# Expert outputs added in DRAM: one output array instead of two, with per-tile waits taken from a table

## What is computed

```python
def _L0_ffn_ref(x, Wr, br, W1, b1, W2, b2):        # E = 8 experts, D = 256, H = 512
    xf = x.reshape(n, d)                             # n = 10368 tokens, after a layer norm
    probs = jax.nn.softmax(xf @ Wr.T + br, axis=-1)
    top2_prob, top2_idx = jax.lax.top_k(probs, 2)
    comb = jnp.zeros((n, e)).at[jnp.arange(n)[:, None], top2_idx].add(top2_prob)
    h = jax.nn.gelu(jnp.einsum('nd,edh->enh', xf, W1) + b1[:, None, :], approximate=False)
    o = jnp.einsum('enh,ehd->end', h, W2) + b2[:, None, :]
    return jnp.einsum('ne,end->nd', comb, o)         # each token: a sum of two weighed rows
...
t = t + _L0_ffn_ref(_ln_t(t), ...)                   # t: the tokens of x1
```

## Time and profile before

| | |
|---|---|
| median of 3 runs | 1621.7 us (1620.54 to 1624.31) |
| the profiled execution | 1627.32 us, its span 1625.6 us |
| until x1 is done | 754.6 us |
| routing stage, to the first tile's load | 754.6 to 1004.7 us |
| expert stage, to the first load of the tail | 1004.7 to 1537.9 us |
| tail: loads and additions, then the output | 1537.9 to 1599.2, to 1625.6 us |
| busy share PE, DVE, ACT, POOL | 81%, 67%, 47%, 35% |

### The profile page before, as it was taken

The page is one execution under the profiler, slowest core; times in us unless marked ns, Lnnn a source line. Parts: engine busy times, 40 slices in busy tenths (PEclk is TensorE's granted clock), DMA queues, the critical chain, the costliest instruction groups (busy, mean ns, idle before and its releaser), DMA issues.

```text
span 1625.6 us, 36996 instructions
## 1 busy us (share of the span) xinstructions
PE 1309.9 (81%) x9796; PEld 1078.3 (66%) x9797; DVE 1087.0 (67%) x2553; ACT 772.1 (47%) x1828; POOL 568.0 (35%) x561
## 2 busy tenths in 40 slices
PE   0196999799999999986746501999999999999692
PEld 0186999756766666666746501888888888888531
DVE  6796555357888877874566662777777777777462
ACT  0294666344445444442576771455554545555200
POOL 0162111134433444330377775233333333333200
PEclk9997999889999999995555555999999999999896
DMA  8535566778778777661144354222222222222297
GB/s 321 139 92 192 202 241 235 252 176 188 188 170 202 179 185 189 162 148 54 54 150 135 131 179 158 76 85 91 91 91 87 84 89 90 90 91 77 85 423 310
DMA packets 258517, 251.16 MB, mean 155 GB/s; under 512 B 150009, under 2 KB 234446, under 8 KB 255204
## 3 DMA queue, kind: packets, MB, share of 16 engines
q1 hardware_dynamic: 238093, 197.20, 41.1%
q0 software_dynamic: 20320, 53.45, 9.6%
q10 hardware_dynamic: 66, 0.05, 0.0%
HBM read 152.34 MB, written 105.75 MB: 159 GB/s over the span
## 4 chain that ended last, share of the span: by engine, by line
PE 59%; DVE 15%; DMA 9%; issue 5%; ACT 5%; SPq 2%; POOL 2%; DVEq 0%; ACTq 0%; POOLq 0%
PE ps L690 15%; PE ps L675 14%; PE ps L490 5%; PE ps L470 4%; DMA u_d<-in_zstrings 3%; PE ps L659 2%; DMA pool_<-y_d 2%; PE ps L542 2%; POOL rows_d L1521 2%; PE ps L515 2%; SPq L288 2%; PE ps L525 2%; DMA pool_<-in_ffn_w 2%; ACT aux L1388 2%; PE ps L459 2%
## 5 line engine op out<-in xcount | busy, mean ns | idle before, releaser
L1530 POOL DMA_INDIRECT y_d<-pool_,to_s x176 | 173.5, 986 | 361.2 <-ACT pool_ L1447 331.9
L690 PE MATMUL ps<-pool_,aux 128*128 x2112 | 248.4, 274 | 6.2 <-DVE aux L1197 3.2
L675 PE MATMUL ps<-aux,pool_ 128*128 128x256 f16 x2112 | 246.5, 274 | 0.7 <-ACT aux L1440 0.6
L690 PEld LDWEIGHTS ps<-pool_,aux 128*128 128x128 f16 x2112 | 199.7, 98 | 49.9 <-issue 25.6
L675 PEld LDWEIGHTS ps<-aux,pool_ 128*128 x2112 | 206.2, 98 | 25.9 <-issue 1.7
L1521 POOL DMA_INDIRECT rows_d<-aux,idx_s x162 | 159.2, 983 | 105.4 <-ACT aux L1390 60.0
L1440 ACT ACTIVATE aux<-ps,b_s 128x256 f32<-128x256 f32 x352 | 138.3, 475 | 93.0 <-DVE aux L1197 92.6
L1432 ACT ACTIVATE aux<-ps 128x512 f16<-128x512 f32 x88 | 52.6, 597 | 188.8 <-PE ps L659 188.8
L1515 POOL DMA_DIRECT2D pool_<-v_d x64 | 50.0, 781 | 223.5 <-PE ps L575 220.3
L1205 DVE SCALAR_TENSOR_TENSOR pool_<-ps,pool_ 128x512 f32<-128x512 f32 x88 | 60.9, 692 | 96.0 <-PE ps L690 96.0
L515 PE MATMUL ps<-pool_,se_w_s 81*81 81x512 f32 x256 | 118.8, 608 | 6.1 <-DMA pool_<-k_d 6.1
(11 more groups left out here) (204 smaller groups left out, 3030.6 us busy)
## 6 DMA issues: line engine op xcount, KB each, us to landing
pool_<-rows_d SPq DMA_DIRECT2D x88, 260.0 KB, 2.8
pool_<-y_d SPq DMA_DIRECT2D x18, 1152.0 KB, 13.9
big<-in_x SPq DMA_DIRECT2D x2, 5184.0 KB, 21.3
xn_d<-big SPq DMA_DIRECT2D x16, 648.0 KB, 3.0
v_d<-aux SPq DMA_DIRECT2D x64, 162.0 KB, 2.1
ks_d<-aux SPq DMA_DIRECT2D x64, 162.0 KB, 2.2
pool_<-xn_d SPq DMA_DIRECT2D x32, 324.0 KB
pool_<-k_d SPq DMA_DIRECT2D x32, 324.0 KB
```

What stands on the lines that cost most here:

```text
L675: last = nc.tensor.matmul(o, w_s[:, a, bass.ds(e * (4 * PIECE) + (k * HID + j * 128), 128)], xh_s[:, par, b, k * SLOTS:(k + 1) * SLOTS], s ...
L690: last = nc.tensor.matmul(ps[:, 6 + par, s * C:(s + 1) * C], hh_s[:, par, a, j, s * 128:(s + 1) * 128], w_s[:, b, bass.ds(e * (4 * PIECE) ...
L1530: nc.gpsimd.indirect_dma_start(out=y_d[:, :], out_offset=bass.IndirectOffsetOnAxis(ap=to_s[:, par, k:k + 1], axis=0), in_=yo_s[:, par, k, ...
```

## The change

- `y_d` has one row for each token and 256 rows for padding (`TOKENS + SLOTS`). Both of a token's rows are added into the same row: the indirect DMA of `return_rows` has `compute_op=ALU.add`, and no bounds check.
- The array has to hold zeros first: ahead of b2 and the weights SP issues two DMAs that write `zero_s`, 1024 bytes a row, over all 10,624 rows of `y_d` (10.88 MB). DVE clears `zero_s` for that at the end of the first half instead of after the routing.
- Two additions to the same row must not be under way together. A token's two experts differ, so a tile waits for all tiles of the experts in front of its own: for each tile two more numbers stand in `tabi_s` (rows 2 and 3, nine more DVE instructions), the counts that `yst0` and `yst1` must have reached, at least 32 each. A tile past the last real one counts as an expert's first. POOL reads both numbers into registers for each tile from the third on, and waits on both semaphores.
- The tail loads one array: 9 loads instead of 18, 27 multiplications on PE instead of 54, and no L1238 on DVE.

The core of the diff:

```diff
-        y_d = dram("y_d", [2 * TOKENS, C])
+        y_d = dram("y_d", [TOKENS + SLOTS, C])
...
             sp.wait_ge(S["x1_c"], GROUPS + CREDIT)
+            sp.wait_ge(S["zero_c"], 1)
+            nought = zero_s[:, 0:1, 0:C]
+            sp.dma_start(y_d[0:TOKENS, :].rearrange("(b q) c -> b q c", q=HW),
+                         nought.to_broadcast([128, HW, C])).then_inc(S["nought"], 16)
+            sp.dma_start(y_d[TOKENS:, :].rearrange("(s b) c -> b s c", b=128),
+                         nought.to_broadcast([128, SLOTS // 128, C])).then_inc(S["nought"], 16)
             sp.dma_start(b2_s, bass.AP(ffn_b2.tensor, 0, [[0, 128], [1, EXPERTS * C]])).then_inc(S["b2_in"], 16)
...
-                for k in range(2):
-                    rows = y_d[k * TOKENS:(k + 1) * TOKENS, :].rearrange("(b q) c -> b q c", q=HW)
-                    sp.dma_start(got_s[:, n % 4, k], rows[:, n * CHUNK_P:(n + 1) * CHUNK_P, :]
-                                 ).then_inc(S[f"gat{n % 4}"], 16)
+                rows = y_d[0:TOKENS, :].rearrange("(b q) c -> b q c", q=HW)
+                sp.dma_start(got_s[:, n % 4, 0], rows[:, n * CHUNK_P:(n + 1) * CHUNK_P, :]
+                             ).then_inc(S[f"gat{n % 4}"], 16)
...
+            nc.vector.memset(zero_s[:, :, :], 0.0).then_inc(S["zero_c"], 1)
+            dve.wait_ge(S["zero_c"], 1)
             link(nc.vector.tensor_copy(base_s[:, :], region_s[:, :]))
...
-            link(nc.vector.memset(zero_s[:, :, :], 0.0))
...
+            starts, halved = tcmp_s[:, 1, :, 0], tcmp_s[:, 1, :, 1]
+            link(nc.vector.scalar_tensor_tensor(starts, tab_s[:, 1, :], -1.0 / SLOTS, turn_s[:, :], ALU.mult, ALU.add))
+            for other in range(2):
+                tiles_landed = tabi_s[:, 2 + other, :]
+                link(nc.vector.tensor_scalar(halved, starts, float(1 - other), 2.0, ALU.add, ALU.max))
+                link(nc.vector.tensor_copy(tiles_landed, halved))
+                link(nc.vector.tensor_scalar(tiles_landed, tiles_landed, 1, None, ALU.arith_shift_right))
+                link(nc.vector.tensor_scalar(tiles_landed, tiles_landed, 5, None, ALU.logical_shift_left))
...
-                nc.vector.scalar_tensor_tensor(to_s[:, par], here_s[:, 1], -float(TOKENS), first,
-                                               ALU.mult, ALU.add).then_inc(S["idx2_c"], 1)
+                nc.vector.tensor_copy(to_s[:, par], first).then_inc(S["idx2_c"], 1)
...
                 pool.wait_ge(S["yw_c"], t + 1)
+                if not isinstance(t, int):
+                    for other in range(2):
+                        landed_of = pool.value_load(tabi_s[0:1, 2 + other, bass.ds(t, 1)], min_val=32, max_val=16 * TILES)
+                        pool.wait_ge(S[f"yst{other}"], landed_of)
                 settle()
                 for k in range(2):
                     nc.gpsimd.indirect_dma_start(
                         out=y_d[:, :], out_offset=bass.IndirectOffsetOnAxis(ap=to_s[:, par, k:k + 1], axis=0),
-                        in_=yo_s[:, par, k, :], in_offset=None, bounds_check=2 * TOKENS - 1, oob_is_err=False).then_inc(S[f"yst{par}"], 16)
+                        in_=yo_s[:, par, k, :], in_offset=None, compute_op=ALU.add).then_inc(S[f"yst{par}"], 16)
-
-            with pool.Fori(0, TILES // 2) as i:
+            pool.wait_ge(S["nought"], 32)
+            pool.wait_ge(S["tab_r"], 1)
+            return_rows(0, 0)
+            pool.wait_ge(S["yst0"], 32)
+            return_rows(1, 1)
+            with pool.Fori(1, TILES // 2) as i:
                 for par in range(2):
                     return_rows(i * 2 + par, par)
```

More of the change, by code:

```diff
@@ L214, in metaformer_kernel @@
         tili_s = sb("tili_s", [128, 2, EXPERTS], i32)
-        tabi_s = sb("tabi_s", [1, 2, TILES], i32)
+        tabi_s = sb("tabi_s", [1, 4, TILES], i32)
         aux_at[0] = 0
@@ L243, in metaformer_kernel @@
                    l2_p l2m_c e_c band_p x1_c phase_a wst_in0 wst_in1 wst_in2 whi_c wlo_c b2_in rm_p rw_c
-                   blk_p part_c turned_c lgr_c var2_c ln_c rstd_c nmr_c probs_c ex2_c tot_c tri_p xft_c idx_c
+                   blk_p part_c turned_c lgr_c var2_c ln_c rstd_c nmr_c probs_c ex2_c tot_c tri_p xft_c idx_c zero_c nought
                    """ + " ".join(f"scat{k}" for k in range(RING)) + """ yw_c ends_c base_c pad_out tab_r rin0 rin1 tt_p xhi_c xlo_c h_p
-                   gel_c hhi_c hlo_c w2_p yo_c tag_c idx2_c yst0 yst1 gat0 gat1 gat2 gat3 sum_p mix_d fin_d
+                   gel_c hhi_c hlo_c w2_p yo_c tag_c idx2_c yst0 yst1 gat0 gat1 gat2 gat3 sum_p fin_d
                    out_s meta_c settle_s"""
@@ L712, in _ @@
             for n in range(HW // CHUNK_P):
-                pe.wait_ge(S[f"gat{n % 4}"], 32 * (n // 4 + 1))
+                pe.wait_ge(S[f"gat{n % 4}"], 16 * (n // 4 + 1))
                 if n >= 2:
@@ L718, in _ @@
                 for bank in range(SUMMED // 2):
[L719 to L722, removed]
+                    last = nc.tensor.matmul(ps[:, 4 * (n % 2) + bank, :], ident_s[:, :],
+                                            got_s[:, n % 4, 0, 2 * bank:2 * bank + 2, :].rearrange("b q c -> b (q c)"),
+                                            start=True, stop=True)
                 last.then_inc(S["sum_p"], 1)
@@ L1233, in _ @@
                 sums, mine = outs[:, :, 0:SUMMED], outs[:, :, SUMMED:CHUNK_P]
-                dve.wait_ge(S[f"gat{n % 4}"], 32 * (n // 4 + 1))
+                dve.wait_ge(S[f"gat{n % 4}"], 16 * (n // 4 + 1))
                 nc.vector.tensor_tensor(mine, mine, got_s[:, n % 4, 0, SUMMED:CHUNK_P, :].rearrange("b q c -> b c q"),
-                                        ALU.add).then_inc(S["mix_d"], 1)
-                dve.wait_ge(S["mix_d"], n + 1)
-                nc.vector.tensor_tensor(mine, mine, got_s[:, n % 4, 1, SUMMED:CHUNK_P, :].rearrange("b q c -> b c q"),
                                         ALU.add)
@@ L1567, in _shape_constants @@
     token = np.zeros((128, HW, 4), np.float32)
-    token[:, :, 1] = TOKENS + np.arange(TOKENS).reshape(BS, HW)
-    pad = 2 * TOKENS + np.arange(SLOTS, dtype=np.float32).reshape(-1, 128).T
+    token[:, :, 1] = np.arange(TOKENS).reshape(BS, HW)
+    pad = TOKENS + np.arange(SLOTS, dtype=np.float32).reshape(-1, 128).T
     order = np.tile(EXPERTS - np.arange(EXPERTS), (128, 1))
```

## The result

The changed kernel takes 1632.27 us in the median of five runs (1630.24 to 1637.89), the kernel before 1623.74 on the same chip (1620.54 to 1625.0). The ratio is 1.0066, with a 95% interval of 1.0048 to 1.0085 (the medians alone give 1.0053): slower by about 0.7%, where 1601.9 us, faster by 1.2%, had been forecast.

The account below looks back on a forecast made before the run. PE's two multiplications were taken to bound the expert stage, with the routing stage and tail also in the chain. Terms -27.7 + 5.3 + 2.6 = -19.8 us from the median 1621.7 gave 1601.9 us, range 1594 to 1608 (0.60).

Parts of the forecast that it names:

- The tail: Final stage summing rows: half the loads and multiplications and L1238 go, 61.36 us becomes 33.7, a gain of 27.7 us.
- The rival of a low clock: Tail: PE keeps clock 0.52, so the tail gains only 8.4 us and the time is 1621; chance 0.06.
- The zeros: Routing stage: zero writes delay the first weight piece, ACT stalls and POOL's second batch is late: +5.3 us, 0 to 15.
- the figures of the Trainium skill: Zero writes at line rate would take 25 us, with no stall and a forecast 5 us lower; weighed but not adopted.
- The end of the stage: Last tile of the expert stage: the tail waits for its landing without cover, so the longer way counts once, +2.6 us.
- The way back of a tile: Expert stage, POOL's two DMAs to landing: 2.6 us longer (loads 1.3, issue 0.3, landing 1.0), of 1.3 to 6.1; 88 tiles free.
- The estimate from the Trainium skill: Extra read of an addition priced by HBM access, 0.2 us average, 2 at high load: way longer by 1.8 to 3.6 us.
- the 3.6 us in hand: Expert stage: slack of a landing, 2.65 us before DVE's destinations plus 0.92 idle before L1205; any delay inside it costs nothing.
- the rule of 43 us for each microsecond: Expert stage: delay over 3.6 us is paid once in two tiles, 43 us for each microsecond.
- The table's waits: Expert stage: an expert's first tile waits for the tile before, which lands by 1305.8, about when its DMA comes: nothing.
- The remark that they would also be free for every tile: Expert stage: even if the counts made every tile wait for the one in front, cost nothing and time 1602.
- The rival that named this place: Way back takes over the expert stage: slower if longer by 4.1 us, about 1713 at the far ends; chance 0.22.

Follow-up runs that it names:

- e1_hoist: Changed kernel with the two register loads and table waits moved ahead of POOL's waits for the tile's own rows: 1622.24 us, ratio 0.9967 to the kernel before.
- e2_plain: Changed kernel with plain writes in place of the additions, leaving out the sum of a token's two rows: 1611.34 us, ratio 0.9912 to the kernel before.
- e3_prev: Changed kernel without the table's loads, every tile waiting for the landing of the tile in front: 1707.94 us, ratio 1.0514 to the kernel before.
- e4_both: Changed kernel with register loads and table waits moved earlier, and zeros issued behind the third weight piece: 1611.05 us, ratio 0.9899 to the kernel before.
- e8_four: Kernel before, with four unused register loads ahead of its two plain writes: expert stage 519.0 us, against 509.5 before.
- e7_two_loads: Kernel before, with rows added into two zeroed halves and two unused register loads, no table waits: expert stage 532.7 us, against 509.5 before.
- e9_seven: Kernel before, with seven unused register loads ahead of its two plain writes: expert stage 581.2 us, against 509.5 before.
- e6_two: Kernel before, with rows added into two zeroed halves, no table, waits or loads: expert stage 515.2 us, against 509.5 before.

## Why the prediction was wrong

**The tail** was right: -27.7 forecast, -27.1 measured, with DVE back to back at 2.6 us a chunk through most of it. That the sum is so near is partly luck: the first chunk took 12.0 us, not 11.3, and the last two stood 1.1 us for loads that had been called no limit (the last landed 29.6 us after the first issue, not 27.5), while DVE's chunk took 2.6 and not 2.8. The rival of a low clock fell: PE was granted 0.50, the lower level, for its first 3.4 us there and 1.00, the upper, from 1580 us on.

**The zeros** were right in mechanism and somewhat too dear: +5.3 forecast; 3.5 us in this profile, 4.2 to 5.0 by `e1_hoist`, `e2_plain` and `e3_prev` against `e4_both`. The rate was that of the earlier trace rows: 347 GB/s at a full share of the DMA engines, 47 engine-us for a MB where 48 had been taken. By the figures of the Trainium skill that the prediction weighed against it ("DMA: Bandwidth & Descriptors", Specifications: 512 bytes as the smallest transfer for line rate, 435 GB/s as the ceiling) there would have been no stall; the trace disagrees, with 1 KB rows at 347 GB/s, and the measurement decides.

**The end of the stage**: +2.6 forecast, +3.6 measured.

**The way back of a tile** is the step that failed, in two of its numbers.

The first is the length of the way, 2.6 us forecast and 3.5 measured (8.03 - 4.56). Of its three items the loads were right: 1.3 forecast, and the first addition follows the weighed rows 1.3 us later than the write did (2.19 against 0.88). The issue was taken at +0.15 us a DMA and is +0.57 (1.86 from one start to the next, against 1.29). The landing was taken at +1.0 from the DMA's start and is +1.6 for a tile's second DMA (medians 3.95 and 2.39). I chose the issue from POOL's direct DMAs, which say that many pieces are cheap; but the addition has the same 128 pieces as the write, and still issues 0.58 us longer. The bounds of 1.3 to 6.1 held the value, the choice near the low end did not. The estimate from the Trainium skill ("DMA: Bandwidth & Descriptors", Latency and other measured facts) took 2 us for the extra read and ended at 3.6. The trace agrees with that far end in the sum alone: the landing is 1.6 us later, and the issue makes up the rest.

The second is the 3.6 us in hand, read as a threshold. It was 2.65 us in front of DVE's destinations plus 0.92 of idle time behind them. Where DVE does wait, the destinations start 0.26 us after the landing, so up to that wait only 2.3 us were in hand (2.56 - 0.26, medians). By the rule of 43 us for each microsecond over it the runs would have lost 0 (`e8_four`, +2.5), 0 (`e7_two_loads`, +3.5) and 87 us (`e9_seven`, +5.6). They lost 9.5, 23.2 and 71.7. The price is there at +1.9 (5.7 us in `e6_two`) and rises steadily; +1.2 is the longest way that was free (0.8 us in `e2_plain`). Part of this shows in `e7_two_loads`: a tile's wait for `y_d` is 46.7 us over 65 tiles, 0.72 us, but the idle time behind it fell only from 1.16 us a tile (`e6_two`, 78.3 over 67) to 0.77, by 0.39. The prediction itself said that the split of the next tile's rows, which PE needs, stands behind that wait; idle time that DVE spends waiting for PE doesn't cover a delay that makes PE late. What costs the first 5 to 9 us, where DVE hardly waits, is open; PE's longer register loads, in `e6_two` and `e8_four` and in the changed kernel too (52 of its 78 inner tiles, ahead of the down product), are a candidate that no run isolates.

**The table's waits** were forecast at nothing and cost some 3.4 us, not much more than two profiles of one program differ by. The remark that they would also be free for every tile was wrong by 94 us (609.5 in `e3_prev` against 515.2 with the additions alone): it set the landing 2.6 us later against the next tile's start, and left out that a wait there feeds its own delay to the next tile. From one tile's first addition to the next it is 1.86 + 4.4 + 0.8 = 7.07 us, more than the 5.87 us of a tile.

Together: 5.7 for the additions, 17.5 for the loads on top of them (532.7 - 515.2), 3.4 for the table, 26.6 us in the expert stage. The rival that named this place had been given 0.22; its place was right and its point of decision, a way longer by 4.1 us, was too far out: the changed kernel is behind at 3.5.

## What to carry to other kernels

Before an operation in a ring of buffers is made slower, follow one buffer all the way round and price each new item on it; only the idle time up to the first wait is in hand, less the time from a release to the start behind it, and here even that was not free to its last microsecond. A releaser named by the profile is the event that came last, not always the one that was waited for: compare the same step in a run without that wait. What needs only early data, such as a register load or a wait for another tile, goes ahead of the wait for late data: the same instructions then cost a fraction. A large fill goes behind the small loads that are due next, in queue order, and must be through before the load behind it is due: 21.2 MB of zeros in the same place cost 27 us (`e6_two`).

## What the runs showed of the hardware

- An indirect DMA of 128 rows of 1 KB from SBUF to DRAM issues on POOL in 0.96 to 0.98 us and lands 2.4 us after its start; with addition 1.56 and 3.8. At 88 to 89 GB/s from 1100 to 1500 us the share of the DMA engines goes from 0.28 to 0.56.
- A register load on POOL takes 0.29 us and 0.15 for the register work behind it, 0.55 us from one to the next; two put the next DMA off by 1.2 us (`e2_plain`) to 1.3 (the changed kernel).
- PE's register load ahead of the up product took 0.30 us (median) in the kernel before and 0.49 in `e6_two`. Why it takes longer is not shown.
- Filling 10.9 MB of DRAM with 1 KB pieces from one SBUF tile went at 347 GB/s, and SP stood 27.85 us in the issue of the second of two such DMAs (256 rows behind 10,368), with everything behind it in its queue.
- Plain writes land late now and then (at most 4.4 us after their start in `e8_four`, where 2.4 is the median); with the way back that long already, that landing held a tile for 2.2 us.
